# Weight preparation moved from ScalarE and GpSimd to VectorE, query and key rows normalised by VectorE out of PSUM, and the narrow branch of TensorE placed first

## The chip, the cores and the metric

The kernel runs on one core of a Trainium2 chip. The metric is the device time of one execution in microseconds (us). The kernel before takes 264.18 us (median of 3 runs, 264.0 to 264.33).

## The reference

Inputs are `x` (16 tiles of 128 rows by 256) and a context of the same shape. Two steps, each added to `x` with a tanh gate:

```
q = layernorm(x) @ Wq.T;  k, v = context @ Wk.T, context @ Wv.T interleaved    # 32 heads of 8
q, k = rmsnorm(q), rmsnorm(k)                    # per row and head, over 8 elements
x = x + tanh(g_xattn) * softmax(q k.T / sqrt(8)) v
h = layernorm(x);  W = (wq - 128) * scale        # int32 weights of gate, up (704x256), down (256x704)
x = x + tanh(g_ffn) * (silu(h Wg.T) * (h Wu.T)) Wd.T
```

## The kernel before

Each engine has a program of its own, in a fixed order, with semaphores between them. The unit of work is an iteration `p` (from -1 to 9), which carries two attention tiles and one pair of tiles of the feed-forward part; each iteration has a half `e = 0` and a half `e = 1`. Iterations 2 to 5 are a hardware loop, the others are written out. In iteration `p` the queries and keys of tiles 2p+2 and 2p+3 are made (iterations -1 to 6), the attention of tiles 2p and 2p+1 is done, and the feed-forward part of the pair p-2 is finished (chunks 2 to 5 of the hidden layer, then the two output products y0 and y1) and that of the pair p-1 begun (chunks 0 and 1).

**PSUM banks.** All projections share three banks. The order in which tasks take them is `TASKS` (L95), and the bank is in `BANK_OF` (L93):

```
BANK_OF = {"out0": 0, "v0": 1, "qk0": 2, "ffn2": 0, "ffn3": 1, "ffn4": 2, "ffn5": 0,
           "out1": 1, "v1": 2, "qk1": 0, "turn2": 1, "y0": 2, "y1": 0, "ffn0": 1, "ffn1": 2}
```

TensorE claims a bank with `claim` (L1071): it waits on `drained[k]` until every earlier task of that bank has been read out. So ffn4 follows qk0 in bank 2, and y1 follows qk1 in bank 0. Where the feed-forward tasks do not exist yet (iterations -1, 0 and 1), v1 follows qk0 in bank 2. In iteration 2 v0 follows ffn0 in bank 1 and qk0 follows ffn1 in bank 2.

**Queries and keys.** TensorE fills a bank with 512 columns (`queries_keys`, L1141). ScalarE squares it (`square`, L583) and copies it to SBUF (`copy_qk`, L594), which drains the bank. VectorE sums the squares per head (L842), runs a chain of eight small root instructions (L809, L736 to L742), and multiplies the copy with the roots into `qk_parts[:, :, 0]` in float16 (`qk_upper`, L855). GpSimd makes the same product in float32 (`qk_norm`, L451) and subtracts the float16 part (`split_qk`, L411) for the lower part. VectorE duplicates the parts (`qk_double`, L867 to L869), and the SP queue turns them with two DMA transposes (L340).

**Feed-forward weights.** They are int32 numbers less 128, kept as a float32r upper part (`gu_hi`, `dn_hi`) and a lower part (`gu_lo`, `dn_lo`) that only the wide branch uses. ScalarE makes the upper parts in iteration 0 (L513, L520, L522) and squares all weights for their maximum in iteration 1 (L535). GpSimd makes the lower parts in iterations 0 and 1 (L460, L462, L472, L474), in front of `add_attention` (L428), which adds the attention to `x` and on whose result VectorE's second layernorm waits (`statistics2`, L905). VectorE reduces the maxima (L973), a DMA turns them into a row (L372), and VectorE writes the flag `wide` (L980). TensorE loads the flag into a register after the attention of iteration 1 and branches (L1302 to L1311): the wide branch comes first in the code, the narrow one is the `Else`. With these inputs the narrow one runs: 8 matmuls for each full chunk.

`roots`, `gate`, `up` and `normalize2` are interleaved on VectorE by hand (L998 to L1062): in half 0, roots 1 to 5, gate 2, root 6, up 2, root 7, gate 3, up 3, then `qk_upper`; in half 1, roots 1 to 4, `turn2_lo` (L943), roots 5 to 7, `normalize2` (L827), then `qk_upper`.

## Time and profile before

| | us |
|---|---|
| median of 3 runs | 264.18 |
| profiled execution | 263.58 |
| its span, first to last instruction | 261.8 |
| TensorE busy | 206.6 (79%) |
| VectorE busy | 172.0 (66%) |
| ScalarE busy | 152.8 (58%) |
| GpSimd busy | 133.0 (51%) |

The profile shows one execution. Times in its rows count from the first instruction. PE is TensorE's matmuls, PEld its weight loads, DVE VectorE, ACT ScalarE, POOL GpSimd, SPq the queue of the DMA issues. The mean granted clock of TensorE is 0.909 of full speed.

### The profile page before, as it was taken

What the parts mean: (1) busy time and instruction counts of PE and PEld (TensorE: products, weight loads), DVE (VectorE), ACT (ScalarE), POOL (GpSimd) and SP (SyncE); (2) the same over time, 40 slices, a digit from 0 to 9 for tenths busy, and PEclk for the clock granted to TensorE, in tenths of its full rate; (3) what the DMA queues carried; (4) which work ended last, traced back from release to release, by engine and by line L of the source; (5) the groups of instructions that cost most, each with busy time, mean ns of one, the idle gap of its engine ahead of it and who ended that gap; (6) DMA issues with size and microseconds to landing.
All of it is one profiled execution on the core that took longest, in us unless ns stands there. A gap on an engine that the chain in (4) does not pass through costs nothing.

```text
span 261.8 us, 6738 instructions
## 1 busy us (share of the span) xinstructions
PE 206.6 (79%) x2388; PEld 162.0 (62%) x2388; DVE 172.0 (66%) x523; ACT 152.8 (58%) x284; POOL 133.0 (51%) x165
## 2 busy tenths in 40 slices
PE   3652966866700899989998999899999999886794
PEld 2441644544500777777777778687877877675784
DVE  2664163787080349795977788687959798576563
ACT  1122477676620378666856775687578767753371
POOL 5043079325929535464728382836375465444472
PEclk9995779596865599999999999999999999999799
DMA  7897505053500050616051605332351405010011
GB/s 235 248 341 170 123 0 123 0 42 82 120 1 3 4 123 0 72 50 160 0 120 21 140 5 115 64 96 49 72 124 44 80 3 123 0 43 1 3 40 40
DMA packets 44021, 20.15 MB, mean 77 GB/s; under 512 B 36384, under 2 KB 41440, under 8 KB 43872
## 3 DMA queue, kind: packets, MB, share of 16 engines
q1 hardware_dynamic: 44000, 19.87, 32.9%
q8 instruction: 13, 0.21, 0.3%
q14 instruction: 8, 0.07, 0.1%
HBM read 9.38 MB, written 2.10 MB: 44 GB/s over the span
## 4 chain that ended last, share of the span: by engine, by line
PE 40%; DVE 27%; issue 10%; POOL 9%; ACT 5%; DMA 5%; SPq 1%; DVEq 1%; POOLq 0%; ACTq 0%
PE bank L1130 10%; PE bank L1225 9%; PE bank L1203 8%; PE pv_ps L1112 7%; DVE silu L918 3%; POOL whole L460 3%; PE score_ps L1093 3%; DMA k_stack<-qk_parts 3%; POOL gu_lo L462 3%; ACT probs L549 3%; DVE hidden L933 2%; DVE sums L842 2%; PE bank L1185 1%; ACT squares L583 1%; POOL qk_parts L411 1%
## 5 line engine op out<-in xcount | busy, mean ns | idle before, releaser
L549 ACT ACTIVATE probs<-score_ps 128x1024 f32<-128x1024 f32 x64 | 64.6, 1023 | 9.7 <-PE score_ps L1093 9.3
L1203 PE MATMUL bank<-x_hi,gu_hi 128*128 128x256 f32 (+1 forms) x192 | 49.4, 294 | 14.4 <-issue 12.9
L451 POOL TENSOR_TENSOR qk_unit<-qk_raw,root_y 128x512 f32<-128x512 f32 x16 | 18.2, 1140 | 78.9 <-DVE root_y L742 78.9
L1112 PE MATMUL pv_ps<-probs,v_blocks 128*32 128x128 f32 x1024 | 43.4, 290 | 13.2 <-ACT probs L549 13.2
L1203 PE MATMUL bank<-x_lo,gu_hi 128*128 128x256 f32 (+1 forms) x192 | 47.5, 284 | 0.0
L1203 PEld LDWEIGHTS bank<-x_hi,gu_hi 128*128 128x128 f32 (+1 forms) x192 | 35.4, 184 | 18.1 <-issue 15.5
L419 POOL TENSOR_TENSOR h_lo<-hidden,h_hi 128x256 fp32r<-128x256 f32 (+1 forms) x48 | 37.3, 788 | 17.5 <-ACT h_hi L633 16.6
L1130 PE MATMUL bank<-w,xc 128*128 128x256 f32 x128 | 41.0, 474 | 5.5 <-DMA w<-qkv_dram 4.4
L622 ACT ACTIVATE tanh_g<-bank,half_gate 128x256 f32<-128x256 f32 (+1 forms) x48 | 22.7, 474 | 29.2 <-PE bank L1203 27.4
L1112 PEld LDWEIGHTS pv_ps<-probs,v_blocks 128*32 128x32 f32 x1024 | 25.3, 113 | 23.2 <-ACT probs L549 14.3
L1130 PEld LDWEIGHTS bank<-w,xc 128*128 128x128 f32 x128 | 28.6, 236 | 14.3 <-issue 7.3
L1203 PEld LDWEIGHTS bank<-x_lo,gu_hi 128*128 128x128 f32 (+1 forms) x192 | 35.5, 185 | 0.0
L918 DVE SCALAR_TENSOR_TENSOR silu<-tanh_g,bank 128x256 f32<-128x256 f32 (+1 forms) x48 | 19.9, 415 | 15.6 <-ACT tanh_g L622 15.4
L1093 PE MATMUL score_ps<-q_stack,k_stack 32*128 32x128 f16 x512 | 22.5, 227 | 8.5 <-DMA k_stack<-qk_parts 8.5
L1093 PEld LDWEIGHTS score_ps<-q_stack,k_stack 32*128 32x128 f16 x512 | 12.8, 97 | 19.8 <-DMA k_stack<-qk_parts 9.2
L905 DVE BATCH_NORM_STATS2 x_stats<-x_all 128x6 f32<-128x256 f32 (+1 forms) x16 | 6.8, 427 | 27.3 <-POOL x_all L428 27.3
L933 DVE SCALAR_TENSOR_TENSOR hidden<-silu,scales,bank 128x256 f32<-128x256 f32 (+1 forms) x48 | 23.0, 479 | 2.6
L1225 PE MATMUL bank<-dn_hi,h_hi 128*128 128x256 f32 x84 | 23.2, 310 | 0.1
L411 POOL TENSOR_TENSOR qk_parts<-qk_unit,qk_parts 128x512 f16<-128x512 f32 x16 | 18.9, 1179 | 7.8 <-DVE qk_parts L855 7.5
L1225 PE MATMUL bank<-dn_hi,h_lo 128*128 128x256 f32 x84 | 21.7, 293 | 0.0
L633 ACT CAST h_hi<-hidden 128x256 fp32r<-128x256 f32 (+1 forms) x48 | 18.2, 404 | 5.7 <-DVE hidden L933 5.1
L842 DVE TENSOR_REDUCE sums<-squares 128x64 f32<-128x512 f32 x16 | 11.0, 686 | 13.0 <-ACT squares L583 12.3
(93 smaller groups left out, 349.2 us busy)
## 6 DMA issues: line engine op xcount, KB each, us to landing
xc<-turned_dram SPq DMA_DIRECT2D x16, 256.0 KB, 2.9
out_dram<-x_all SPq DMA_DIRECT2D x16, 128.0 KB, 1.9
x_all<-x_dram SPq DMA_DIRECT2D x1, 1536.0 KB, 10.6
gu_int<-gate_up_dram SPq DMA_DIRECT2D x1, 1280.0 KB, 5.9
w<-qkv_dram SPq DMA_DIRECT2D x3, 256.0 KB, 3.4
dn_int<-down_w_dram SPq DMA_DIRECT2D x1, 640.0 KB, 7.1
x_all<-x_dram SPq DMA_DIRECT2D x1, 384.0 KB, 5.1
q_stack<-qk_parts SPq DMA_TRANSPOSE x16, 3.2
```

The lines of the kernel that those rows point to most:

```text
L411: nc.gpsimd.tensor_tensor(qk_parts[:, :, 1, :], qk_unit[:], qk_parts[:, :, 0, :], ALU.subtract).then_inc(qk_lo_ready, 1)
L419: nc.gpsimd.tensor_tensor(h_lo[0:r, j, :], hidden[0:r, j % 3, :], h_hi[0:r, j, :].bitcast(F32), ALU.subtract).then_inc(h_lo_ready, 1)
L451: nc.gpsimd.tensor_tensor(qk_unit[:], qk_raw[:], root_y[:, 0:2 * H].unsqueeze(2).to_broadcast([P, 2 * H, HD]), ALU.mult).then_inc(unit_rea ...
L549: nc.scalar.activation(probs[:, t % 2, :], score_ps[t % 2][:].rearrange("p h n -> p (h n)"), ACT.Exp, scale=float(HD) ** 0.5 / UNIT ** 2). ...
L622: nc.scalar.activation(tanh_g[0:r, j % 2, :], bank[k][0:r, 0:TOK], ACT.Tanh, scale=half_gate[0:r, j:j + 1]).then_inc(tanh_g_ready, 1)
L918: nc.vector.scalar_tensor_tensor(out=silu2[0:r, j % 2, :], in0=tanh_g[0:r, j % 2, :], scalar=1.0, in1=bank[k][0:r, 0:TOK], op0=ALU.add, op ...
L933: nc.vector.scalar_tensor_tensor(out=hidden[0:r, j % 3, :], in0=silu2[0:r, j % 2, :], scalar=scales[0:r, 2, j:j + 1], in1=bank[k][0:r, TOK ...
L1093: last = nc.tensor.matmul(score_ps[t % 2][:, s, :], k_stack[of, e, g, :], q_stack[of, e, g, :], start=True, stop=True, tile_position=(BLOC ...
L1112: last = nc.tensor.matmul(pv_ps[BLOCK * quadrant:BLOCK * (quadrant + 1), region * P:(region + 1) * P], v_blocks[:, e, h * BLOCK:(h + 1) * ...
L1130: last = nc.tensor.matmul(dst, xc[:, tile, source, c, :], weights[:, c, :], start=(c == 0), stop=(c == KC - 1))
L1203: last = nc.tensor.matmul(bank[k][0:r, a * TOK:(a + 1) * TOK], w[:, j, a, c, 0:r], xx[:, c, :], start=(n == 1), stop=(n == (4 if wide_weig ...
L1225: last = nc.tensor.matmul(bank[k][:, 0:D], hh[:, j, e * P:(e + 1) * P], w[:, j, :], start=(n == 1), stop=(n == (4 if wide_weights else 2) ...
```

## The change

- VectorE makes the product of queries and keys with the roots once, in float32, reading the PSUM bank (`qk_rows`), in the place where `qk_upper` stood; this instruction now drains the bank. `copy_qk`, `qk_norm` and the buffer `qk_raw` go. ScalarE copies the result to float16 (new `qk_upper`), in half 0 behind tanh of chunk 4, in half 1 behind `drain_y(p, 1)`. GpSimd only subtracts.
- All weight work but the squares is VectorE's. Upper parts: chunks 0 to 2 around `qk_rows(-1, 1)`, chunks 3 to 5 and the down weights in `begin(0)`. Lower parts: one fused instruction each instead of two, chunks 0 to 3 in iteration 0, 4 and 5 in iteration 1 behind `qk_rows`, the down weights in iteration 1 in front of `gate(1, 0)`. The squares stay on ScalarE, and all six run at the end of iteration -1.
- The maximum and the flag are made in `begin(0)`, its DMA is issued in iteration 0 behind `stacks(0, 0)`. The load of `x` tiles 4 to 15 moves behind iteration -1 of the SP queue.
- TensorE's branch has the narrow case first.

```diff
@@ SP
-            sp.dma_start(x_all[:, 4:B, :], x[4:B].rearrange("b p d -> p b d")).then_inc(x_loaded[2], 16)
+            def load_widest():
+                sp.wait_ge(w_max_steps, 1)
+                sp.dma_start(weight_max_row[:], weight_max[:, 6:7]).then_inc(w_max_row_loaded, 16)
             def iteration(p):
                 stacks(p, 0)
+                if p == 0:
+                    load_widest()
...
                 load_rows(p, 0)
-                if p == 1:
...
+                if p == FIRST:
+                    sp.dma_start(x_all[:, 4:B, :], x[4:B].rearrange("b p d -> p b d")).then_inc(x_loaded[2], 16)
@@ GpSimd
                 pool.wait_ge(qk_hi_ready, b + 3)
-                pool.wait_ge(unit_ready, b + 3)
                 nc.gpsimd.tensor_tensor(qk_parts[:, :, 1, :], qk_unit[:], qk_parts[:, :, 0, :],
@@ GpSimd, iteration
-                qk_norm(p, 0)
                 split_chunks(p, 2, (2,))
                 split_qk(p, 0)
                 split_chunks(p, 2, (3, 4, 5))
-                if isinstance(p, int) and p in (0, 1):
-                    for j in range(3 * p, 3 * p + 3):
-                        lower_gate_up(j)
                 add_attention(p, 1)
-                qk_norm(p, 1)
                 split_qk(p, 1)
-                if isinstance(p, int) and p == 1:
-                    for i in range(4):
-                        lower_down(i)
@@ ScalarE
-            def copy_qk(p, e):
+            def qk_upper(p, e):
...
-                    act.wait_ge(filled[k], m)
+                    act.wait_ge(drained[k], m)
                     if since(b, -1):
-                        act.wait_ge(unit_ready, b + 2)
-                        act.wait_ge(qk_hi_ready, b + 2)
-                    nc.scalar.copy(qk_raw[:].rearrange("p h d -> p (h d)"), bank[k][:]).then_inc(drained[k], 1)
+                        act.wait_ge(stacked, 32 * (b + 2))
+                    nc.scalar.copy(qk_parts[:, :, 0, :], qk_unit[:]).then_inc(qk_hi_ready, 1)
@@ ScalarE, iteration
                 square(p, 0)
                 exp_octet(p, 0, 2)
-                copy_qk(p, 0)
...
                 tanh_chunk(p, 2, 4)
                 if ending(p):
                     upper(p, 2, 3)
+                qk_upper(p, 0)
                 drain_pv(p, 1)
                 exp_octet(p, 1, 0)
...
                 square(p, 1)
-                copy_qk(p, 1)
+                if isinstance(p, int) and p == FIRST:
+                    act.wait_ge(rest_zeroed, 1)
+                    for i in range(6):
+                        square_weights(i)
...
                 exp_octet(p, 1, 3)
                 drain_y(p, 1)
+                qk_upper(p, 1)
                 tanh_chunk(p, 1, 0)
@@ VectorE
-            def qk_upper(p, e):
+            def qk_rows(p, e):
...
                 dve.wait_ge(root_steps, (ROOT_STEPS + 1) * (b + 3))
-                k, m = use(p, f"qk{e}")
-                dve.wait_ge(drained[k], m)
                 if since(b, -1):
-                    dve.wait_ge(stacked, 32 * (b + 2))
-                nc.vector.tensor_tensor(qk_parts[:, :, 0, :], qk_raw[:], root_y[:, 0:2 * H].unsqueeze(2).to_broadcast([P, 2 * H, HD]),
-                                        ALU.mult).then_inc(qk_hi_ready, 1)
+                    dve.wait_ge(qk_lo_ready, b + 2)
+                k, _ = use(p, f"qk{e}")
+                nc.vector.tensor_tensor(qk_unit[:], bank[k][:].rearrange("p (h d) -> p h d", d=HD),
+                                        root_y[:, 0:2 * H].unsqueeze(2).to_broadcast([P, 2 * H, HD]),
+                                        ALU.mult).then_inc(drained[k], 1)
+            def convert_gate_up(j):
...
+                nc.vector.tensor_scalar(gu_hi[:, j, :, :, 0:rows(j)], source, ZERO_POINT, None,
+                                        ALU.subtract).then_inc(gu_hi_ready, 1)
+            def convert_down():
...
+                for j0, j1, r in DOWN_PARTS:
+                    nc.vector.tensor_scalar(dn_hi[0:r, j0:j1, :], dn_int[0:r, j0:j1, :], ZERO_POINT, None,
+                                            ALU.subtract).then_inc(dn_hi_ready, 1)
+            def lower_gate_up(j):
...
+                nc.vector.scalar_tensor_tensor(out=gu_lo[:, j, :, :, 0:rows(j)], in0=source, scalar=-ZERO_POINT,
+                                               in1=gu_hi[:, j, :, :, 0:rows(j)].bitcast(F32), op0=ALU.add,
+                                               op1=ALU.subtract).then_inc(lo_ready, 1)
@@ VectorE, begin and iteration
+                if isinstance(p, int) and p == 0:
+                    widest_weight()
+                    for j in (3, 4, 5):
+                        convert_gate_up(j)
+                    any_wide_weight()
+                    convert_down()
...
-                qk_upper(p, 0)
+                qk_rows(p, 0)
+                if second:
+                    lower_gate_up(0)
+                    lower_gate_up(1)
+                if third:
+                    lower_gate_up(4)
+                    lower_gate_up(5)
...
-                qk_upper(p, 1)
+                if first:
+                    convert_gate_up(0)
+                    convert_gate_up(1)
+                qk_rows(p, 1)
+                if first:
+                    convert_gate_up(2)
                 if second:
-                    x_statistics(2, 10, B)
-                    x_means(3)
...
+                    lower_gate_up(2)
+                    lower_gate_up(3)
+                if third:
+                    qk_double(p, 2)
+                    for i in range(4):
+                        lower_down(i)
                 gate(p, 1, 0)
@@ TensorE
-            with pe.If_ne(any_wide, 0):
+            with pe.If_eq(any_wide, 0):
+                first_chunks(1, False)
+                run(pe, lambda p: iteration(p, False), FIRST_STEADY)
+            with pe.Else():
                 first_chunks(1, True)
                 run(pe, lambda p: iteration(p, True), FIRST_STEADY)
-            with pe.Else():
-                first_chunks(1, False)
-                run(pe, lambda p: iteration(p, False), FIRST_STEADY)
```

In iteration 0 (`second`) the statistics of tiles 10 to 15 move behind `qk_double(p, 2)`. `wait_for_root_buffers` waits on the drained bank where it waited on `unit_ready`.

## Rows read from the trace of the kernel before

**Rows 1.** Busy time by window, one steady period: window, length, engines' busy us (count), PEclk, DMA, GB/s.

```profile
117.55:142.25 24.70, 23.60 (x302) 18.74 (x298) 19.74 (x56) 17.77 (x34) 13.67 (x17) 1.00 0.34 74
```

**Rows 2.** The chain that ended last, in order of time: start us, us, what.

```profile
11.71 0.70 DVE sums L842
14.81 1.58 POOL qk_unit L451
...
81.02 4.63 issue
85.65 3.75 PE bank L1203 x16
...
95.83 0.61 ACT squares L583
...
112.80 1.88 PE bank L1203 x16
```

**Rows 3.** Timeline of PE, iteration 3: start us, us, what.

```profile
124.22 0.38 PE L1203 MATMUL bank<-x_hi,gu_hi 128*128 128x256 f32 x1
...
135.82 0.39 PE L1225 MATMUL bank<-dn_hi,h_hi 128*128 128x256 f32 x1
```

**Rows 4.** Timeline of ACT, iteration 3.

```profile
120.53 0.60 ACT L583 ACTIVATE squares<-bank 128x512 f32<-128x512 f32 x1 [0.59 <-PE bank L1130]
...
121.94 0.59 ACT L594 COPY qk_raw<-bank 128x512 f32<-128x512 f32 x1
```

**Rows 5.** Timeline of DVE, iteration 3.

```profile
125.78 1.09 DVE L855 TENSOR_TENSOR qk_parts<-qk_raw,root_y 128x512 f16<-128x512 f32 x1
...
133.38 0.69 DVE L842 TENSOR_REDUCE sums<-squares 128x64 f32<-128x512 f32 x1
...
137.21 1.28 DVE L827 TENSOR_SCALAR x1n<-x_all,x_mean_var,root_y 128x256 f32 x1
138.41 0.68 DVE L855 TENSOR_TENSOR qk_parts<-qk_raw,root_y 128x512 f16<-128x512 f32 x1
```

**Rows 6.** One line's or one tile's instructions: duration ns min/median/max, first and last start.

```profile
L943 DVE TENSOR_TENSOR x_lo<-bank,x_hi x8: 683/691/692, 75.2 to 246.3; 128x512 fp32r<-128x512 f32 x8
L827 DVE TENSOR_SCALAR x1n<-x_all,x_mean_var,root_y x16: 401/826/1277, 50.6 to 243.1; 128x256 f32<-128x256 f32 x8, 128x256 f32 x8
L535 ACT ACTIVATE weight_squares<-gu_int x3: 622/1075/1080, 56.4 to 62.9; 128x1024 f32<-128x1024 int32 x2, 128x512 f32<-128x512 int32 x1
L535 ACT ACTIVATE weight_squares<-dn_int x2: 407/845/1283, 69.4 to 70.7; 128x1280 f32<-128x1280 int32 x1, 64x256 f32<-64x256 int32 x1
```

**Rows 7.** Timeline of POOL up to 72 us.

```profile
36.13 1.16 POOL L411 TENSOR_TENSOR qk_parts<-qk_unit,qk_parts 128x512 f16<-128x512 f32 x1
...
71.60 0.73 POOL L428 TENSOR_TENSOR x_all<-x_all,attn 128x256 f32<-128x256 f32 x1
```

**Rows 8.** Timeline of PE up to 75 us.

```profile
12.21 3.78 PE L1130 MATMUL bank<-w,xc 128*128 128x256 f32 x8 [1.16 <-ACT qk_raw L594]
15.78 1.09 PE L1130 MATMUL bank<-wq_centred,xc 128*128 128x256 f32 x4
...
72.14 0.65 PE L1112 MATMUL pv_ps<-probs,v_blocks 128*32 128x128 f32 x16 [2.05 <-ACT probs L549]
```

**Rows 9.** Waits of one engine for another: us in total, times, longest.

```profile
DVE wide_max L978 <- DMA weight_max_row<-weight_max: 2.0, 1, 2.0
```

**Rows 10.** Timeline of SP's queue.

```profile
25.84 1.23 SPq L340 DMA_TRANSPOSE q_stack<-qk_parts  x1
```

**Rows 11.** Busy time by window, as in Rows 1, around two low stretches of TensorE.

```profile
59.00:61.00 2.00, 0.20 (x8) 0.00 (x0) 1.76 (x8) 0.91 (x3) 0.00 (x0) 0.82 0.82 196
...
72.00:73.00 1.00, 0.65 (x16) 0.38 (x16) 0.60 (x2) 1.00 (x3) 0.34 (x1) 1.00 0.02 8
```

**Rows 12.** Timeline of the end, all engines.

```profile
257.89 0.28 PE L1243 MATMUL bank<-dn_hi,h_lo 128*128 128x256 f32 x1
...
259.15 0.81 SPq L361 DMA_DIRECT2D out_dram<-x_all  x2
```

More of the change, by code:

```diff
@@ L142, in build_program @@
         dn_int = sb("dn_int", [P, NJ, D], I32)
-        whole = sb("whole", [P, 2 * D])
         gu_hi = sb("gu_hi", [P, NJ, 2, KC, P], F32R)
@@ L532, in square_weights @@
                              (LAST, dn_int[0:LAST, NJ - 1, :]))[i]
+                if i == 0:
+                    act.wait_ge(ffn_w_loaded[0], 16 * 2)
+                if i == 4:
+                    act.wait_ge(ffn_w_loaded[1], 16 * 2)
                 if i > 1:
@@ L661, in iteration @@
             def iteration(p):
-                def early(q, work, *args):
-                    if isinstance(p, int) and p == q:
-                        work(*args)
                 square(p, 0)
                 exp_octet(p, 0, 2)
-                copy_qk(p, 0)
-                early(0, convert_gate_up, 0)
-                early(1, square_weights, 0)
                 if not (isinstance(p, int) and p == PAIRS + 1):
@@ L774, in _, with wait_for_root_buffers @@
             x_means(0)
-            def wait_for_root_buffers(p, b):
+            def wait_for_root_buffers(p, e):
+                b = 2 * p + e
                 if has_tile(p, b - 1):
@@ L780, in wait_for_root_buffers @@
                 if since(b, -1) and has_tile(p, b + 1):
-                    dve.wait_ge(unit_ready, b + 2)
+                    k, m = use(p, "qk0") if e else use(p - 1, "qk1")
+                    dve.wait_ge(drained[k], m)
                 if since(b, 2):
@@ L791, in root_inputs @@
                 if not has_tile(p, b + 2):
-                    wait_for_root_buffers(p, b)
+                    wait_for_root_buffers(p, e)
                 if has_tile(p, b - 1):
@@ L968, in scale_setup, with lower_down @@
                 nc.vector.tensor_scalar(down_scale[:], down_scale[:], tanh_gates[:, 1:2], None, ALU.mult).then_inc(scale_steps, 1)
+            def convert_gate_up(j):
+                if j == 0:
+                    dve.wait_ge(ffn_w_loaded[0], 16 * 2)
+                source = gu_int[:, j] if j < NJ - 1 else gu_int_rest[:]
+                nc.vector.tensor_scalar(gu_hi[:, j, :, :, 0:rows(j)], source, ZERO_POINT, None,
+                                        ALU.subtract).then_inc(gu_hi_ready, 1)
+            def convert_down():
+                dve.wait_ge(ffn_w_loaded[1], 16 * 2)
+                dve.wait_ge(rest_zeroed, 1)
+                for j0, j1, r in DOWN_PARTS:
+                    nc.vector.tensor_scalar(dn_hi[0:r, j0:j1, :], dn_int[0:r, j0:j1, :], ZERO_POINT, None,
+                                            ALU.subtract).then_inc(dn_hi_ready, 1)
+            def lower_gate_up(j):
+                source = gu_int[:, j] if j < NJ - 1 else gu_int_rest[:]
+                dve.wait_ge(gu_hi_ready, j + 1)
+                nc.vector.scalar_tensor_tensor(out=gu_lo[:, j, :, :, 0:rows(j)], in0=source, scalar=-ZERO_POINT,
+                                               in1=gu_hi[:, j, :, :, 0:rows(j)].bitcast(F32), op0=ALU.add,
+                                               op1=ALU.subtract).then_inc(lo_ready, 1)
+            def lower_down(i):
+                j0, j1, r = DOWN_PARTS[i]
+                dve.wait_ge(dn_hi_ready, i + 1)
+                nc.vector.scalar_tensor_tensor(out=dn_lo[0:r, j0:j1, :], in0=dn_int[0:r, j0:j1, :], scalar=-ZERO_POINT,
+                                               in1=dn_hi[0:r, j0:j1, :].bitcast(F32), op0=ALU.add,
+                                               op1=ALU.subtract).then_inc(lo_ready, 1)
             def widest_weight():
@@ L1001, in iteration @@
                 second = isinstance(p, int) and p == FIRST + 1
+                third = isinstance(p, int) and p == 1
                 sum_squares(p, 0)
@@ L1060, in iteration @@
                 up(p, 1, 1)
-                qk_double(p, 2)
+                if not third:
+                    qk_double(p, 2)
+                if second:
+                    x_statistics(2, 10, B)
+                    x_means(3)
                 begin(p + 1)
```

69 lines of the change are left out of this document (3 added, 66 removed).

## The prediction

> **What bounds the kernel now.** I read the page first (engine shares), then busy time by window, then the chain of waits, then the timelines of single engines. Two regimes show. From iteration 2 on TensorE is the bound: in a steady period of 24.70 us it is busy 23.60 us at full granted clock, while VectorE works 19.74, ScalarE 17.77 and GpSimd 13.67 [rows 1]. Little can be hidden from TensorE there: 1.1 us. Up to 95.8 us the bound is latency. The chain has 4.63 us of "issue" from 81.02 to 85.65, when TensorE, done with the attention of iteration 1 at 72.8 [rows 8], has its flag and takes the branch [rows 2]; the first two chunks behind it run slow, 3.75 us for 16 matmuls that take 1.88 later [rows 2]. Before that, GpSimd's weight work holds back `add_attention`, to 71.60 in iteration 1 [rows 7].
>
> So the change has two sums: what it saves up to the point where ScalarE squares the queries and keys of iteration 2, now at 95.83 [rows 2], and what it adds to each of the five iterations 2 to 6 that make queries and keys beside the feed-forward part.
>
> **Steady iterations, half 0.** Today ScalarE's copy frees the bank of qk0 at 121.94 + 0.59 = 122.53 [rows 4]. The next task of that bank is ffn4, and TensorE begins it at 124.22 [rows 3], 1.7 us later: the bank is never waited for. After the change `qk_rows` frees it, and it needs the whole root chain. It stands where `qk_upper` stands, at 125.78 [rows 5]. VectorE works without a gap from the sums to there, and nothing before it becomes shorter. Its duration: a product of 512 columns with one operand in PSUM takes 0.69 (x_lo [rows 6]); today's `qk_upper` from SBUF takes 0.68 undisturbed and 1.09 here [rows 5], where GpSimd works beside it. I take 0.69, as x_lo is 0.69 at all 8 places; the bounds are 0.68 and 1.09. The bank is free at 126.47, ffn4 begins at 126.5 and not 124.22: +2.28 us (bounds 2.2 to 2.7). Everything behind it on TensorE's queue moves: attention of the next tile, ffn5, v1 and qk1, and so ScalarE's square of qk1 from 131.69 to 133.97. The cover that copy_qk gave is gone and nothing takes its place, since TensorE executes in order.
>
> **Steady iterations, half 1.** qk1 frees bank 0 for y1, which begins at 135.82 [rows 3]; with +2.28 that is 138.1. The VectorE side: ScalarE's upper copy of half 0 runs behind tanh of chunk 4, about 128.2 to 128.8 (a 512-column copy is 0.59 [rows 4]), GpSimd's subtraction to 130.0 (1.16 [rows 7]). gate and up of chunk 5, the three doubling copies, the division and GpSimd's addition of the attention follow, and the sums begin at about 135.1, not 133.38 [rows 5]: less than +2.28 later, as VectorE lagged by some 0.5 there. From the sums to the end of the roots 3.83 pass (133.38 to 137.21 [rows 5], with turn2_lo inside). Then the normalisation: 1.28 today, beside GpSimd's float32 product, 0.40 undisturbed [rows 5, 6]; that product is gone, so 0.40. `qk_rows(p, 1)` runs at 139.3 to 140.0, and y1 begins at 140.05: another +1.9 us (bounds 1.3 to 2.8, the upper one if the normalisation keeps 1.28). ScalarE's copy of half 1 fits in the 0.6 us between draining y1 and the tanh of chunk 0. The transposes start within 1 us of where they do now relative to the period, 5 us ahead of the scores that need them. The period becomes 24.70 + 2.28 + 1.9 = 28.9 us. Over five iterations: 5 x 4.16 = +20.8 us (bounds 18 to 25). The rest, iterations 7 to 9, has no qk tasks and keeps its length.
>
> **The first iterations.** Here each engine's queue has to be followed; every time below is the largest of what the instruction waits for, with durations of before. A root chain without normalisation is 3.1 from sums to product [rows 2].
> - Iteration -1: qk0 is full at 11.0 as now, the product runs 14.76 to 15.45. v1 needs that bank: TensorE starts it at 15.5, not 12.21 [rows 8]. Behind the idle time the 12 matmuls are mostly slow (8 took 3.57, the next 4 1.09 [rows 8]): qk1 is full at about 20.5. ScalarE squares it and then all weights, six instructions and their accumulator reads, 4.8 us (1.075 x 2 + 0.62 + 0.40 + 1.28 + 0.41 less overlap, [rows 6]), to 25.8. VectorE: sums 21.15, roots 24.15, two conversions. A one-operand conversion of 512 columns from int32 is in no row on VectorE; bounds 0.40 (the 256-column normalisation, undisturbed) and 0.69 [rows 6]; I take 0.55. `qk_rows(-1, 1)` ends near 26.0, ScalarE's copy at 26.6, and only then comes the first exp, at 26.6 in place of 23.9.
> - Iteration 0: qk0 full at 33.3. On VectorE `begin(0)` stands in front of its sums: the doubling ends at 28.5, conversions to 30.2, then the flag's DMA, which SP issues behind two transposes (1.23 each and more [rows 10]) at 31.1 and which takes 2.0 [rows 9] (behind the landing of the transposes up to 2 more): 33.2, then the flag and four conversions to 35.9. Sums 2 us late, product to 39.65. ScalarE waits with its upper copy for it, and behind the copy in its queue stand the drain of pv and the exps of tile 1: exp at 40.65. v1 and qk1: full at 47.3. In return GpSimd's addition follows the division at once (47.1), and sums(0, 1) start at 48.0. The product ends at 52.35, ScalarE copies to 53.0, and the exps of iteration 1 stand behind that: 53.35. qk0 of iteration 1 full at 60.0, the product at 64.6, exps of the second tile at 65.6, qk1 full at 72.0.
> - Iteration 1, end: the attention was added long before (69.2, today 72.3 [rows 7]), so sums(1, 1) start at 72.75, today 72.83. turn2_lo ends at 75.9 and chunk 0 can start there: the flag has been known since 34. Were the 4.63 of load and branch paid in full from 74.2, it would be 78.8; the narrow case now follows the branch directly, so I take 76. The product ends at 77.7, copy 78.35, subtraction 79.55, doubling 80.2, and then four lower parts of the down weights, 0.69 x 2 + 0.41 x 2 = 2.2 (two operands, as x_lo; bound above 1.49 each, were they as slow as GpSimd, +3): gate 0 at 82.4, up 0 to 83.3, up 1 to 84.2. v0 of iteration 2 waits for bank 1 (up 0), qk0 for bank 2 (up 1): full at 86.4.
>
> So the square of iteration 2 comes at 86.4 in place of 95.83: -9.4 us. The 10 us saved at chunk 0 are not more than this since VectorE's lower parts stand in front of gate 0. A slow clock or a slow branch at 76 is hidden behind them. Bounds -6 (conversions and lower parts at the dear end, flag late) to -12.
>
> **The end.** The narrow body now has the wide one behind it, and TensorE has to jump over it after its last matmul at 258.2 [rows 12]. At the price of today's jump, 4.63 [rows 2], it ends at 262.8, against 261.8 for the last store, whose issue is at 259.15 and later [rows 12]: +1.0 (bounds 0 and 1.0).
>
> **Sum.** 263.58 (profiled execution) - 9.4 + 20.8 + 1.0 = 276.0. The median of the runs is 0.6 above the profiled one, which is in the rounding: 276 us.
>
> **Rivals.**
> - *The stalls cost the clock.* After each stall TensorE may run at 1.2 GHz. For it: the clock was granted at 0.82 on average in 59 to 61, with 0.20 us of work there [rows 11]. Against: after the 2.05 us idle up to 72.14 the products run in 0.65 and the granted clock is 1.00 [rows 8, 11], and dense matmuls stand on both sides of my stalls of 2.3 and 1.9. Price: 16 matmuls lose 1.87 [rows 2]; one fall per iteration makes 276 + 9.4 = 285, two make 295. The Trainium skill, "TensorE: Matmul & The Clock Gate", section "Why this matters for your kernels", wants no idle gap over about 3 us between bursts; by that rule neither stall would cost the clock, and the time stays 276. The trace agrees with it at 72.14; at 59 to 61 the clock fell behind gaps of about 2 us in a thin stretch, which the rule does not tell.
> - *The stalls are hidden (the other side).* If ffn4 and y1 met a free bank, only the start and the end would count: 263.58 - 9.4 + 1.0 = 255. The mechanism would be a shorter VectorE chain, with GpSimd's product gone. The point from which it decides is a stall of 1.7 us per iteration in all: (9.4 - 1.0) / 5. For it: VectorE loses up to 0.9 us per half to GpSimd's work beside it. Against: that contention lies behind the sums only in half 1, where I have taken it out; in half 0 the gap from 122.53 to 126.47 is 3.9 us and TensorE has 1.7 us of slack.
> - *The first iterations gain nothing.* ScalarE's upper copy waits for VectorE in front of the exps, and all its delays add up in iterations -1 to 1: were the four steps each 2 us dearer, chunk 0 would come at 84 and the time would be 285.
>
> **How the numbers follow.** Forecast 0.68, clock 0.13, hidden stalls 0.06, no gain at the start 0.07; 0.06 for what I have not seen, spread over both sides. Own range of the forecast: all cheap ends together give 263.58 - 12 + 18 + 0 = 270, all dear ones 263.58 - 6 + 25 + 1 = 284; as they will hardly meet, 271 to 282. For 8 in 10 I widen it to 268 to 285, up to the first clock fall. A change within 0.2% (0.5 us) cannot be told from none. Faster takes the hidden stalls and a little of the rest, 0.06; same 0.02; slower 0.92.
>
> **What would show it.** The wait of ffn4 and of y1 on `qk_rows` as idle time of TensorE of some 2 us each in iterations 2 to 6, and a period near 28.9 between their qk0. Chunk 0 at about 76, the square of iteration 2 near 86, no "issue" of 4.6 in front of it, and such a piece at the end. ScalarE's exps of iterations 0 and 1 right behind its upper copies. Granted clock 1.00 from iteration 2 on. It is wrong if the period stays below 26.4 us, or if the square of iteration 2 comes before 83 or after 91.

## The result and the profile after

| | before | after |
|---|---|---|
| median of the runs | 264.09 us (263.96 to 264.33) | 281.78 us (279.6 to 282.53) |
| profiled execution / its span | 263.58 / 261.8 us | 282.23 / 280.4 us |
| ScalarE's square of q and k, iteration 2 | 95.83 | 84.83 |
| the same, iterations 3 to 6 | 120.53, 145.24, 169.92, 194.31 | 114.03, 144.75, 175.37, 205.65 |

The changed kernel takes 1.0655 [1.0594, 1.0717] times as long: slower, by 17.7 us. The forecast was 276.0 (268 to 285), so the time lies inside the range, 5.8 us above the forecast.

The two rows of the page of the changed kernel that say most, busy time and the clock by slice:

```profile
PE 212.9 (76%) x2388; PEld 166.2 (59%) x2388; DVE 166.3 (59%) x543; ACT 149.0 (53%) x276; POOL 88.7 (32%) x129
PEclk9997777687889999979997999989997979999799
```

GpSimd, which the change relieves, shows it (88.7 us busy in place of 133.0), and so does something that I did not forecast: slices with clock digit 7 in the steady part, where the kernel before has 9 throughout. By period of the changed kernel (window, length, engines' busy us, clock), to hold against [rows 1]:

```profile
84.83:114.03 29.20, 23.51 (x306) 18.82 (x300) 17.36 (x55) 17.61 (x34) 11.20 (x16) 1.00 0.20 41
114.03:144.75 30.72, 25.02 (x306) 19.93 (x300) 17.38 (x55) 17.92 (x34) 10.90 (x15) 0.94 0.27 60
144.75:175.37 30.62, 24.93 (x306) 19.84 (x300) 17.41 (x55) 17.91 (x33) 10.88 (x15) 0.94 0.29 59
175.37:205.65 30.28, 24.80 (x302) 19.67 (x298) 17.40 (x55) 17.91 (x33) 10.81 (x15) 0.94 0.27 57
```

The first period has full clock and is 4.5 us longer than before, all of it idle time of TensorE: 5.7 us of it here, 1.1 in [rows 1]. The next three have 1.1 to 1.5 us on top, and in them TensorE is *busy* 1.3 to 1.5 us longer with the same work. So a period pays twice: for two waits, and for a clock fall. The waits of the changed kernel (who waits at which line <- for whom: us in total, times, longest):

```profile
PE bank L1211 <- DVE qk_unit L785: 12.6, 5, 2.6
PE bank L1189 <- DVE qk_unit L785: 11.1, 5, 2.2
PE bank L1116 <- DVE qk_unit L785: 4.5, 1, 4.5
DVE wide_max L941 <- DMA weight_max_row<-weight_max: 4.0, 1, 4.0
```

L1189 is ffn4, L1211 is y1, both waiting for `qk_rows`; L1116 is v1 of iteration -1. What VectorE did up to the release, in iteration 4 (its timeline):

```profile
150.01 0.68 DVE L785 TENSOR_TENSOR qk_unit<-bank,root_y 128x512 f32<-128x512 f32 x1
...
164.98 0.41 DVE L758 TENSOR_SCALAR x1n<-x_all,x_mean_var,root_y 128x256 f32 x1
165.31 0.68 DVE L785 TENSOR_TENSOR qk_unit<-bank,root_y 128x512 f32<-128x512 f32 x1
```

and TensorE at the same places, with iteration 2 ahead of it:

```profile
90.83 0.39 PE L1189 MATMUL bank<-x_hi,gu_hi 128*128 128x256 f32 x1 [2.24 <-DVE qk_unit L785]
91.94 0.64 PE L1098 MATMUL pv_ps<-probs,v_blocks 128*32 128x128 f32 x16
...
150.75 0.56 PE L1189 MATMUL bank<-x_hi,gu_hi 128*128 128x256 f32 x1 [2.24 <-DVE qk_unit L785]
152.73 1.08 PE L1098 MATMUL pv_ps<-probs,v_blocks 128*32 128x128 f32 x16
...
166.05 0.39 PE L1211 MATMUL bank<-dn_hi,h_hi 128*128 128x256 f32 x1 [2.60 <-DVE qk_unit L785]
```

The product takes 0.68 reading PSUM, the normalisation 0.41 in place of 1.28 [rows 5]. Both waits of 2.24 us are alike, but behind that of iteration 2 the 16 small products (one row, x16) take 0.64 and behind that of iteration 4 they take 1.08. The granted clock in the 2 us behind each wait (windows of the changed kernel; the third number from the end is the clock), ffn4 and y1 of iterations 2, 3 and 6:

```profile
90.83:92.83 2.00, 2.00 (x32) 1.58 (x32) 0.47 (x2) 0.71 (x2) 0.00 (x0) 1.00 0.00 0
104.61:106.61 2.00, 2.00 (x17) 2.00 (x18) 0.00 (x0) 0.21 (x1) 0.00 (x0) 1.00 0.00 0
120.03:122.03 2.00, 2.00 (x10) 1.77 (x10) 0.27 (x1) 0.00 (x0) 0.00 (x0) 0.51 0.00 0
135.33:137.33 2.00, 2.00 (x17) 2.00 (x18) 0.00 (x0) 0.21 (x1) 0.00 (x0) 1.00 0.00 0
...
211.60:213.60 2.00, 2.00 (x20) 1.75 (x24) 0.27 (x1) 0.39 (x2) 0.00 (x0) 0.66 0.00 0
226.44:228.44 2.00, 2.00 (x9) 2.00 (x10) 0.00 (x0) 0.00 (x0) 0.00 (x0) 0.50 0.00 0
```

0.5 is the 1.2 GHz level. It falls behind ffn4's wait in iterations 3 to 6 and behind y1's in iteration 6 alone. (Behind ffn4 of iteration 6 it falls within the 2 us, hence 0.66.)

**The account of 280.4 - 261.8 = 18.6 us**, from the squares in the table: start -11.0; periods of iterations 2 to 5 +4.50, +6.01, +5.94, +5.89; from the square of iteration 6 to the attention product that opens iteration 7 +7.17 (25.56, before 18.39); the rest +0.1.

The first iterations and the end, on TensorE, VectorE and ScalarE of the changed kernel:

```profile
75.08 0.36 PE L1189 MATMUL bank<-x_hi,gu_hi 128*128 128x256 f32 x1 [1.70 <-DVE x_lo L874]
...
78.23 1.05 PE L1098 MATMUL pv_ps<-probs,v_blocks 128*32 128x128 f32 x16
81.02 0.64 PE L1098 MATMUL pv_ps<-probs,v_blocks 128*32 128x128 f32 x16 [0.51 <-ACT probs L492]
```

```profile
24.96 0.76 DVE L906 TENSOR_SCALAR gu_hi<-gu_int 128x512 fp32r<-128x512 int32 x2
...
78.94 1.95 DVE L929 SCALAR_TENSOR_TENSOR dn_lo<-dn_int,dn_hi 128x512 fp32r<-128x512 int32 x4
80.82 0.40 DVE L849 SCALAR_TENSOR_TENSOR silu<-tanh_g,bank 128x256 f32<-128x256 f32 x1
81.25 0.48 DVE L864 SCALAR_TENSOR_TENSOR hidden<-silu,scales,bank 128x256 f32<-128x256 f32 x1
```

```profile
39.23 0.62 ACT L536 CAST qk_parts<-qk_unit 128x512 f16<-128x512 f32 x1 [3.68 <-DVE qk_unit L785]
...
79.74 1.95 ACT L492 ACTIVATE probs<-score_ps 128x1024 f32<-128x1024 f32 x2
...
84.83 0.60 ACT L526 ACTIVATE squares<-bank 128x512 f32<-128x512 f32 x1 [0.65 <-PE bank L1116]
```

```profile
276.69 0.76 DVE L883 TENSOR_TENSOR y_sb<-bank,down_scale 128x256 f32<-128x256 f32 x2 [2.04 <-PE bank L1229]
```

Chunk 0 begins at 75.08 in place of 85.65 [rows 2], waiting for x_lo and for no branch. The wait of 4.0 us for the flag's DMA, shown above, delays VectorE's sums of iteration 0 (35.47, where ScalarE's square was done at 33.71), and ScalarE, whose upper copy now needs the product behind these sums, stands idle for 3.68 us in front of it, with the drain of the attention and the exps of the next tile behind. At the end the last drain begins at 276.69 and the span ends 3.7 us later; before, it was 3.8 (258.0 to 261.8): TensorE's jump over the second body shows nowhere.

### The profile page after: what moved, and what is told of

The parts are those of the page before. It is cut to its first block, busy times and chain, and to the rows that moved or that the text cites. A ratio compares the mean times of both kernels' runs of the same rounds, so it can differ in the third digit from the quotient of the medians.

```text
span 280.4 us, 6665 instructions
## 1 busy us (share of the span) xinstructions
PE 212.9 (76%) x2388; PEld 166.2 (59%) x2388; DVE 166.3 (59%) x543; ACT 149.0 (53%) x276; POOL 88.7 (32%) x129
## 4 chain that ended last, share of the span: by engine, by line
PE 28%; issue 28%; DVE 24%; POOL 9%; ACT 7%; DMA 2%; DVEq 1%; POOLq 0%; SPq 0%; ACTq 0%
PE bank L1116 9%; PE bank L1211 6%; PE bank L1189 5%; POOL h_lo L421 4%; PE pv_ps L1098 4%; POOL x_all L430 2%; DVE silu L849 2%; DVE qk_unit L785 2%; DVE sums L773 2%; POOL qk_parts L413 2%; ACT probs L492 2%; DVE hidden L864 2%; DMA w<-qkv_dram 2%; ACT weight_squares L478 1%; DVE attn L826 1%
## 5 line engine op out<-in xcount | busy, mean ns | idle before, releaser
L1189 PE MATMUL bank<-x_hi,gu_hi 128*128 128x256 f32 (+1 forms) x192 | 51.8, 304 | 14.2 <-DVE qk_unit L785 11.1
L1098 PE MATMUL pv_ps<-probs,v_blocks 128*32 128x128 f32 x1024 | 45.1, 299 | 9.7 <-ACT probs L492 9.6
L1189 PE MATMUL bank<-x_lo,gu_hi 128*128 128x256 f32 (+1 forms) x192 | 49.8, 294 | 0.0
L421 POOL TENSOR_TENSOR h_lo<-hidden,h_hi 128x256 fp32r<-128x256 f32 (+1 forms) x48 | 34.4, 728 | 45.6 <-ACT h_hi L575 45.4
L1189 PEld LDWEIGHTS bank<-x_hi,gu_hi 128*128 128x128 f32 (+1 forms) x192 | 37.0, 193 | 18.6 <-DVE qk_unit L785 12.4
L1116 PE MATMUL bank<-w,xc 128*128 128x256 f32 x128 | 40.0, 464 | 8.8 <-DVE qk_unit L785 4.5
L1116 PEld LDWEIGHTS bank<-w,xc 128*128 128x128 f32 x128 | 27.9, 231 | 17.5 <-DVE qk_unit L785 5.2
L1189 PEld LDWEIGHTS bank<-x_lo,gu_hi 128*128 128x128 f32 (+1 forms) x192 | 37.4, 195 | 0.0
L1211 PE MATMUL bank<-dn_hi,h_hi 128*128 128x256 f32 x84 | 24.2, 321 | 12.7 <-DVE qk_unit L785 12.6
L1211 PEld LDWEIGHTS bank<-dn_hi,h_hi 128*128 128x128 f32 x84 | 17.4, 207 | 16.1 <-DVE qk_unit L785 13.9
L1211 PE MATMUL bank<-dn_hi,h_lo 128*128 128x256 f32 x84 | 22.4, 300 | 0.0
L549 ACT COPY y_sb<-bank 128x256 f32<-128x256 f32 x14 | 5.2, 373 | 28.5 <-PE bank L1211 28.5
```

Of the source, the lines that this page charges most:

```text
L421: nc.gpsimd.tensor_tensor(h_lo[0:r, j, :], hidden[0:r, j % 3, :], h_hi[0:r, j, :].bitcast(F32), ALU.subtract).then_inc(h_lo_ready, 1)
L1098: last = nc.tensor.matmul(pv_ps[BLOCK * quadrant:BLOCK * (quadrant + 1), region * P:(region + 1) * P], v_blocks[:, e, h * BLOCK:(h + 1) * ...
L1116: last = nc.tensor.matmul(dst, xc[:, tile, source, c, :], weights[:, c, :], start=(c == 0), stop=(c == KC - 1))
L1189: last = nc.tensor.matmul(bank[k][0:r, a * TOK:(a + 1) * TOK], w[:, j, a, c, 0:r], xx[:, c, :], start=(n == 1), stop=(n == (4 if wide_weig ...
L1211: last = nc.tensor.matmul(bank[k][:, 0:D], hh[:, j, e * P:(e + 1) * P], w[:, j, :], start=(n == 1), stop=(n == (4 if wide_weights else 2) ...
```

## Experiments

Each time is a median of four executions with the lowest and the highest, and the ratio is to the kernel before, measured beside it: 264.03 us beside the first four, 263.24 beside the next four, 263.67 beside the last two. The changed kernel's 281.78 was measured beside 264.09, so a difference to it is uncertain by the 0.8 us that the kernel before moved, besides the spread of the runs. Traces show one execution each. Line numbers differ a little from kernel to kernel.

**1. Take one path back: ScalarE drains the bank again.**

```diff
+ScalarE: copy_qk(p, e): wait filled; qk_raw <- bank; drained += 1   # shortened, as in the edits below
 def qk_rows(p, e):
-    qk_unit <- bank[k] * root_y      # then_inc(drained[k])
+    qk_unit <- qk_raw * root_y       # then_inc(unit_ready)
```

> The changed kernel, but ScalarE again copies queries and keys out of PSUM and drains the bank (where it did before), and qk_rows reads the copy; ScalarE's float16 copy stays. Theory 'bank': TensorE's two waits per iteration (2.2 and 2.2 to 2.6 us, iterations 2 to 6) and the granted clock below 1.00 behind them come from the bank that qk_rows frees late. Then they all go: periods of 24.7 us again, 281.8 - 22.3 (four periods) - 7.2 (iteration 6) = 252 us, and v1 of iteration -1 starts 3 us earlier, so 248 to 254. Rival 'queue': the longer period comes from ScalarE's upper copy, which waits for VectorE in front of other work in ScalarE's queue. Then the copy back changes little, 275 to 285, and the periods stay near 30.

Measured: 251.64 us (250.22 to 253.37), 0.9517 [0.9446, 0.9588]. Its periods from 83.51 on (windows), and VectorE's product in one of them:

```profile
83.51:108.25 24.74, 23.31 (x306) 18.64 (x300) 17.31 (x55) 18.33 (x35) 10.54 (x15) 1.00 0.21 41
108.25:133.25 25.00, 23.48 (x306) 18.80 (x300) 17.81 (x56) 18.42 (x35) 10.96 (x15) 1.00 0.34 76
```

```profile
138.50 0.90 DVE L798 TENSOR_TENSOR qk_unit<-qk_raw,root_y 128x512 f32<-128x512 f32 x1
```

The period is back at 24.6 to 25.0 and the clock at 1.00, with VectorE still making the rows, the product still behind the roots, and ScalarE's upper copy still waiting for it (15 times, 20.1 us in all). So the loss of the steady part is neither VectorE's load nor the order of its queue: it is when the bank comes free, and the clock falls hang on the same waits.

**2. The branch alone** (the kernel before, with the narrow body first).

```diff
-with pe.If_ne(any_wide, 0):  wide body
-with pe.Else():              narrow body
+with pe.If_eq(any_wide, 0):  narrow body
+with pe.Else():              wide body
```

> The kernel before with the narrow branch first and nothing else. Theory 'jump': of the 4.63 us between flag and first chunk most is the taken branch. Then chunk 0 starts at about 81.5 in place of 85.65 and the time is about 260 us, with nothing given back at the end (the changed kernel shows 3.7 us from the last y_sb product to the end, as the kernel before does 3.8). Rival 'load': the 4.63 is the register load from SBUF and the branch costs little. Then 264 us as before.

Measured: 259.98 us (259.12 to 260.51), 0.9841 [0.9779, 0.9903]. The chain of work that ended last, in order of time:

```profile
80.65 1.98 DMA weight_max_row<-weight_max
83.11 1.04 issue
84.16 3.46 PE bank L1203 x16
```

From the end of the flag's DMA to the first matmul 1.5 us pass (82.63 to 84.16); before, they were 5.1, the 4.63 of [rows 2] and some 0.5 ahead of it. The order of two bodies is worth 3.6 us there, 4.1 in the median (the interval of the ratio lies wholly below 1), and nothing of it is given back at the end: from the last drain to the end 3.7 us pass. The Trainium skill, "Runtime: NRT & Kernel Launch", section "Instruction fetch mechanics", says that a taken branch to code outside the window already fetched makes the engine wait for a fetch. The 3.6 us agree with it; that it is a fetch, no row here shows.

**3. The weight work alone** (all of the change but the path of the query and key rows).

```diff
+POOL:    qk_norm(p, e): qk_unit <- qk_raw * root_y
+ScalarE: copy_qk(p, e): qk_raw <- bank; drained += 1
-ScalarE: qk_upper(p, e): qk_parts[.., 0] <- qk_unit
 VectorE, in qk_rows(p, e):
-    qk_unit <- bank[k] * root_y
+    qk_parts[.., 0] <- qk_raw * root_y
```

> All of the change but the path of queries and keys: weight work on VectorE, squares early, flag early, narrow branch first, with ScalarE's copy, VectorE's float16 product and GpSimd's float32 product as before. Theory 'bank': the gain of the first iterations (11.0 us in the changed kernel up to the square of iteration 2) stays and nothing is lost afterwards: 264.1 - 11 = 253, a little less as v1 of iteration -1 need not wait: 249 to 254 us. If the gain at the start needs the new path (GpSimd and ScalarE less loaded), it is smaller: 256 to 260.

Measured: 249.8 us (248.78 to 251.84), 0.9485 [0.941, 0.9561]. One period of it:

```profile
106.52:131.10 24.58, 23.47 (x306) 18.61 (x300) 19.75 (x56) 17.77 (x33) 13.93 (x18) 1.00 0.37 79
```

The square of iteration 2 comes at 81.80, the period is that of before. This is the version to keep: it beats both kernels, by 14.2 and by 32 us. (Experiment 1 at 251.64 lies close to it; their runs overlap.)

**4. The query and key path alone** (the kernel before with `qk_rows` and the upper copy on ScalarE; GpSimd's weight work and the wide body first stay).

```diff
-POOL: qk_norm(p, e)          ScalarE: copy_qk(p, e)
+VectorE: qk_rows(p, e)       ScalarE: qk_upper(p, e)
```

> The kernel before with the new path of queries and keys only (VectorE's product out of PSUM, ScalarE's upper copy, GpSimd subtracts); weight work and branch as before. Theory 'bank': the loss of iterations 2 to 6 is all here, 22.3 + 7.2 = 29.5 us, and iterations -1 to 1 lose some more by v1's wait for the bank: 292 to 299 us. Theory 'queue' gives the same here; it is told apart by the kernel with the copy back.

Measured: 294.67 us (292.0 to 296.16), 1.1184 [1.1102, 1.1266]: +30.6 us. With the -14.2 of experiment 3 the parts add up to 280.4, against 281.8 measured for both. One part gains 14, the other loses 31. Its first two periods are 29.13 and 30.58 us, as in the changed kernel. I had expected the first iterations to lose some more by v1's wait. In the trace (an execution of 292.0 us, the fastest of the four) they do not: the square of iteration 2 comes at 95.94, before at 95.83, and all of the loss lies behind it.

**5. Shorten one of the two waits.** In half 0 VectorE had the gate and up of chunk 3 between the roots and the product.

```diff
                     roots(p, 0, 7, 7)
+                    qk_rows(p, 0)
                     gate(p, 2, 3)
                     up(p, 2, 3)
-                qk_rows(p, 0)
```

> The changed kernel with qk_rows(p, 0) directly behind root 7, in front of gate 3 and up 3 of chunk 3 (0.84 us of VectorE). Theory 'bank': TensorE's wait in front of chunk 4 falls from 2.24 to 1.4 us in iterations 2 to 6, -4.2 us: 277.5 us if the clock still falls behind it. If that wait was what let the clock fall (chunk 4 in 1.98 us against 1.14), the slow stretch goes too, another 1.5 us in four of the iterations: 271 to 273. Rival 'VectorE's chain sets the period whatever the place': gate 3 and up 3 are only pushed behind, 280 to 282.

Measured: 276.73 us (276.2 to 277.42), 1.0503 [1.0444, 1.0562], 5.0 below the changed kernel. In the traces 2.4 us of this lie ahead of iteration 2, where the order of VectorE's work is unchanged: the square comes at 82.38 and not at 84.83, and no run shows why. From that square to the end 192.0 us pass and not 195.6, so the move is worth 3.6. TensorE at ffn4 and y1 of iteration 3, and the clock behind them:

```profile
116.19 0.38 PE L1191 MATMUL bank<-x_hi,gu_hi 128*128 128x256 f32 x1 [1.53 <-DVE qk_unit L785]
...
130.00 0.38 PE L1213 MATMUL bank<-dn_hi,h_hi 128*128 128x256 f32 x1 [2.60 <-DVE qk_unit L785]
```

```profile
116.19:118.19 2.00, 2.00 (x32) 1.60 (x32) 1.25 (x4) 0.68 (x2) 0.32 (x1) 1.00 0.00 0
130.00:132.00 2.00, 2.00 (x14) 2.00 (x15) 0.00 (x0) 0.00 (x0) 0.00 (x0) 0.78 0.00 0
```

The wait shrank by 0.7 us in each of the five iterations, which is all of the 3.6, as a term of the sum should. The clock gave nothing back, against the 271 to 273 us expected for that case. It no longer fell behind ffn4 in iterations 3 and 4, but it fell behind y1 in iterations 3, 5 and 6, and in iteration 5 behind ffn4 too (0.72, after a wait of 1.52); it fell behind neither in iterations 2 and 4. The periods are 28.5, 30.0, 28.4 and 32.4 us.

**6. Keep the waits, fill them.** Eight float32 matmuls of 128 x 128 into an unused part of PSUM in front of ffn4 and of y1; they add work that no output uses.

```diff
+                if j == 4 and has_tile(p, 2 * p + 2):
+                    fill(8)
                 k = claim(p, f"ffn{j}")
...
+                if e == 1 and has_tile(p, 2 * p + 3):
+                    fill(8)
                 k = claim(p, f"y{e}")
```

> The changed kernel with eight extra matmuls of TensorE (128x128 float32, into 128 columns of PSUM that nobody reads) in each of its two waits for qk_rows, in iterations 2 to 6. They take no bank and fit in the wait (about 8 x 0.14 to 0.2 us = 1.1 to 1.6 of 2.2 us). Theory 'clock': iterations 3 to 6 are 1.5 us longer than iteration 2 because the granted clock falls behind the wait. Then it stays at 1.00, chunk 4 takes 1.14 us, all periods are near 29.2: 281.8 - 1.5 x 4 - 1.4 = 274 to 275.5 us. Rival: the extra 1.5 us are another delay (a queue, a contention), then 281 to 283, or above where the extra matmuls don't fit.

Measured: 273.7 us (273.07 to 274.86), 1.0394 [1.0334, 1.0454]: 8.1 us *faster* than the changed kernel, with 80 matmuls more (each stands as two records in the trace). TensorE at the place of the wait, and two periods:

```profile
146.03 2.05 PE L1178 MATMUL pv_ps<-ident,averaging 128*128 128x128 f32 x16
148.34 0.39 PE L1197 MATMUL bank<-x_hi,gu_hi 128*128 128x256 f32 x1 [0.25 <-DVE qk_unit L786]
```

```profile
113.19:142.34 29.15, 27.41 (x338) 22.46 (x332) 17.43 (x55) 17.61 (x34) 10.90 (x15) 1.00 0.29 63
142.34:171.47 29.13, 27.40 (x338) 22.46 (x332) 17.42 (x55) 17.61 (x34) 10.90 (x15) 1.00 0.30 63
```

The first three periods are 29.13 to 29.15 us, the fourth 28.95, all at full clock. The eight products took 2.05 us, more than the 1.1 to 1.6 that I had expected, and still fit in the wait. The price of the waits without the clock is 29.14 - 24.70 = 4.4 us. The price of the clock is read from the two traces: from the square of iteration 2 to the opening of iteration 7 this kernel needs 7.3 us less (139.06, changed 146.38). The other 1.8 us between the spans (271.3 and 280.4) are no part of it: 0.8 lie ahead of that square, and 1.0 behind iteration 6, where the changed kernel has a late clock fall that the kernel before has too.

**7. The changed kernel with the wide body first again.** My prediction had said that a slow branch at 76 us would be hidden behind VectorE's lower parts.

```diff
-            with pe.If_eq(any_wide, 0):
+            with pe.If_ne(any_wide, 0):
```

> The changed kernel with the wide branch first again, as before the change, so that TensorE has to jump; the flag is still early. The kernel with the narrow branch first alone gained 4.1 us where the flag was late. Here the load and the jump begin at 72.8 us and chunk 0 would start near 77.4 in place of 75.1, at the lower clock. Theory 'hidden': gate 0 starts at 80.8 whatever TensorE does, as the lower parts of the down weights stand in front of it, so 281.8 to 282.5 us, no more than 0.5 us longer. Rival: all of the 4 us shows, 286.

Measured: 287.5 us (286.0 to 289.85), 1.0884 [1.0801, 1.0967]: 5.7 us slower than the changed kernel. "Hidden" falls. Its TensorE, ScalarE and VectorE around the branch:

```profile
78.51 0.55 PE L1189 MATMUL bank<-x_hi,gu_hi 128*128 128x256 f32 x1 [4.01 <-issue]
...
82.19 1.08 PE L1098 MATMUL pv_ps<-probs,v_blocks 128*32 128x128 f32 x16
...
85.13 0.64 PE L1098 MATMUL pv_ps<-probs,v_blocks 128*32 128x128 f32 x16 [0.64 <-ACT probs L492]
```

```profile
83.86 1.94 ACT L492 ACTIVATE probs<-score_ps 128x1024 f32<-128x1024 f32 x2
...
88.68 0.60 ACT L526 ACTIVATE squares<-bank 128x512 f32<-128x512 f32 x1 [0.59 <-PE bank L1116]
```

```profile
81.93 0.41 DVE L849 SCALAR_TENSOR_TENSOR silu<-tanh_g,bank 128x256 f32<-128x256 f32 x1
```

This run came to the branch 1.1 us later (ScalarE's last square ahead of it at 72.01, not 70.89). VectorE's gate 0 is later by just that (81.93 against 80.82): it did hide the branch. TensorE shows it all the same: it idles for 4.01 us in front of chunk 0, and the two chunks then take 3.7 us and not 3.1, as less of them runs at full clock. The attention product behind chunk 1 is 3.96 us later (82.19 against 78.23), the exps 4.1, the second product 4.1 (85.13 against 81.02), and the square 3.85. The path that shows is the one through TensorE's queue, attention behind two chunks, and I had not followed it. The two spans differ by 7.6 us (288.0 and 280.4; the profiled execution was the slowest of its four). Behind the square the first two periods are longer by another 4.2, 31.9 and 32.2 us at a mean clock of 0.89 (29.2 and 30.7 at 1.00 and 0.94 in the changed kernel): the clock falls again, in other places. The stretches behind them give 0.4 back.

**8. Move the flag's wait out of the way.** The weight work alone (experiment 3), with VectorE's last conversions and the wait for the flag's DMA behind the upper part of iteration 0.

```diff
 VectorE, iteration 0
-    convert(3..5), wait flag, convert_down      # in begin(0)
     ...
     qk_rows(0, 0)
-    lower_gate_up(0), (1)                       # now with (2), (3), in half 1
+    convert(3..5), wait flag, convert_down
```

> The kernel with the weight part only (249.8 us), and in it the conversions of chunks 3 to 5 and of the down weights and the wait for the flag's DMA behind VectorE's qk_upper(0, 0) in place of in front of the sums of iteration 0; the lower parts of chunks 0 and 1 move to those of 2 and 3. In the weight-only kernel the sums stand about 4 us behind ScalarE's squares there, waiting for the flag's DMA. If that wait is on the path it gains 2 to 3.5 us: 246.5 to 248. If iteration 0 is set by ScalarE's squares of the weights and the transposes instead, 249.5 to 250.

Measured: 250.34 us (249.42 to 250.68), 0.9482 [0.943, 0.9534], against 249.8 for experiment 3. No gain: VectorE's wait for the flag, 6.15 us in the kernel of experiment 3, is not on the path there. This does not carry over to the changed kernel, with its wait of 4.0 us: there ScalarE's exps stand behind the upper copy, which waits for VectorE. What its wait costs, no run shows.

**9. Fill only the wait of ffn4.**

> The changed kernel with 8 extra 128x128 products only in the first stall of an iteration (before ffn4), none in front of y1. The products add work that no output uses. In the changed kernel the clock fell to 1.2 GHz behind the first stall in four of five iterations and behind the second in one. Theory A (a fall belongs to the stall in front of it, the 2.6 us of the second stall is safe wherever it stands between dense products of 128 rows): the four falls of some 1.5 us go, 281.8 - 6 = 275.8, range 275 to 276.7, and the granted clock behind y1's stall stays 1.00 in iterations 2 to 5. Theory B (a stall of this length is at the edge, and which one falls hangs on where it lies in time): the falls move, behind y1's stall in two or more of the first four iterations, 277 to 281.

Measured: 282.45 us (279.88 to 282.79), 1.0674 [1.06, 1.0749]. Theory A falls altogether. Of theory B the sign came, falls behind y1 in two or more of the first four iterations, and the time did not: 282.45 lies above its 277 to 281. The 2 us behind y1's wait, iterations 2, 3, 4 and 6 of this kernel:

```profile
104.77:106.77 2.00, 2.00 (x17) 2.00 (x18) 0.00 (x0) 0.21 (x1) 0.00 (x0) 1.00 0.00 0
...
134.02:136.02 2.00, 2.00 (x9) 2.00 (x10) 0.00 (x0) 0.00 (x0) 0.00 (x0) 0.50 0.00 0
...
164.73:166.73 2.00, 2.00 (x9) 2.00 (x10) 0.00 (x0) 0.00 (x0) 0.00 (x0) 0.50 0.00 0
...
225.39:227.39 2.00, 2.00 (x12) 2.00 (x13) 0.00 (x0) 0.00 (x0) 0.00 (x0) 0.67 0.04 8
```

In iterations 3 to 5 each fall that no longer came behind ffn4 came behind y1 instead, 14 us later, and in iteration 6 y1's was hit as before; behind ffn4 the clock was 1.00 in iterations 2 to 5. So the wait of 2.6 us that looked safe in the changed kernel is not safe in itself. Nor does a fall behind ffn4 simply spare y1: in iteration 6 of the changed kernel both were hit, in iteration 2 neither.

**10. Fill only the wait of y1.**

> The changed kernel with 8 extra products only in the second stall (before y1), none in front of ffn4; they add work that no output uses. Theory A: the first stall's four falls stay, the one fall behind the second goes: 281.8 - 1.5 = 280.3, range 279.5 to 281. Theory B (the place in time decides): the falls behind the first stall come in other iterations, 1 to 5 of them, so anything from 276 to 282; two or fewer of the five would speak for B.

Measured: 279.96 us (279.03 to 281.69), 1.0614 [1.054, 1.0687]. The clock fell behind ffn4 in iterations 3 to 6 and behind y1 never. The time lies in A's range of 279.5 to 281 and in B's of 276 to 282, and it does not speak for A, since experiment 9 has refuted it; B's sign, two or fewer falls, did not come either. With both results, one open wait of 2.1 to 2.6 us per iteration is enough for one fall in each of iterations 3 to 6, and filling one of the two leaves four falls of five.

## Why the prediction was right, and where it missed

**Direction and mechanism: right.** The forecast waits of ffn4 and y1 on `qk_rows`, some 2 us each, came as 2.24 and 2.60 us; the square of iteration 2 came at 84.83 inside its window of 83 to 91; the period is far beyond 26.4. Experiments 1, 3 and 4 separate the two sums: +30.6 for one part alone, -14.2 for the other. They also answer two of the rivals: the stalls were not hidden (255 us), and the first iterations gained 11.0 us and not nothing (285 us).

**Steady part: the two waits.** Measured 4.50 per iteration at full clock, 4.16 forecast, so 22.3 over the five (4 x 4.50, and 4.3 in iteration 6, where they are 2.10 and 2.21) for 20.8. The durations were right (product 0.68, normalisation 0.41, and the 3.83 from sums to roots to the digit: 99.71 to 103.54); the sums of half 1 came 14.88 behind the square and not 14.57. VectorE had the attention ready at 96.99, but GpSimd, with three lower parts of the hidden chunks in front, added it only at 98.14. +1.5 us.

**Steady part: the clock, the term I had at zero.** "Granted clock 1.00 from iteration 2 on" was wrong in iterations 3 to 6. This was my first rival, at 0.13, and it happened in part: five falls of the ten waits, at 1.5, 1.4, 1.4 and, for the two of iteration 6, 2.9 us: 7.2 us in the account, 7.3 by the traces of experiment 6. I had priced one at 1.87. My argument against it was the full clock behind 2.05 us of idle time [rows 8, 11] and dense products on both sides. One row was a sample of one: the changed kernel itself shows a wait of 2.24 us without a fall (iteration 2) and with one (iterations 3 to 5). And the products right in front of both waits are attention products of 32 columns, as at 87.95 and 132.09, with dense ones only behind. Whether that matters, no run shows. The Trainium skill, "TensorE: Matmul & The Clock Gate", section "Why this matters for your kernels", which I had set beside this rival, wants no idle gap over about 3 us. None of these waits is over 2.6 us, and yet the clock fell in four of five iterations: the trace disagrees with the rule, and the measurement decides.

**The first iterations: -11.0, forecast -9.4.** Chunk 0 at 75.08 (forecast 76), no 4.6 us of issue. Conversions take 0.42 each and not 0.55, lower parts 0.68 as forecast; VectorE had the flag at 34.0, forecast 33.2. The 1.6 us beyond the forecast grew in small steps: ScalarE's squares came 0.2, 0.8, 0.6 and 1.1 us before the forecast in iterations 0 and 1, and 1.6 us before it in iteration 2. The step that failed is "A slow clock or a slow branch at 76 is hidden behind them". Experiment 7 shows 2.75 us at the square (3.85 less the 1.1 of the later start) for a branch of 4.0 us and the slower products behind it. In the changed kernel the two paths meet: VectorE's first `hidden` ends at 81.73, the attention product at 81.66. I had computed the first and called it the only one.

**The end: 0, forecast +1.0.** The price of the branch before chunk 0, 4.63 us, was carried over to the end without a row for it. From the last drain to the end 3.7 us pass, as before.

**Sum.** 276.0 + 1.5 + 7.2 - 1.6 - 1.0 + 0.1 = 282.2, the profiled execution's 282.23. That the time fell inside the range is partly luck. Without the clock the terms measured give 275.0 us, which is the forecast's own mechanism and nearly its number; 7.2 us came from a term that stood at zero. The range of 268 to 285 was widened up to the first clock fall, so it covered this; the inner range of 271 to 282 had no clock in it at all, and 281.8 lies in it only because it allowed for dear conversions, flags and waits that did not come.

## What to carry to other kernels

Look for what a drain of a PSUM bank really releases: the cheap copy of 0.6 us by another engine was not wasted work but what kept a 4-us chain of small VectorE operations off TensorE's path; removing it cost 31 us, while the rest of the change gained 14. A wait of 2 us that is added to a TensorE-bound loop should be priced with a clock fall on top, here about one per iteration and not one per wait: of ten waits five were hit, and of the five left by filling the others four. When a step is said to be hidden behind one engine, follow the other queues over the same stretch too, the delayed engine's own first.

## What the hardware showed that I had not expected

- The clock. Of ten waits of 2.1 to 2.6 us five were followed by a fall in the changed kernel; of the five left with y1's filled, four; of the five left with ffn4's filled, four; with both filled, none. Equal waits in equal surroundings differed (iteration 2 against 3). What decides which one is hit stays open. A wait of some 1.5 us (experiment 5) was not hit in three of four iterations, and in the fourth the clock was 0.72 behind it.
- More work made the kernel faster: 80 matmuls whose result nobody reads, -8.1 us between the medians; in the traces 7.3 us in the iterations with the waits.
- The order of two bodies behind a branch was worth 4.1 us before and 5.7 after (of these, in the traces, some 2.75 at the branch and the rest in slower iterations behind it); the jump at the end cost nothing that the rows show.
- VectorE read 512 float32 columns from PSUM with a broadcast operand in 0.68 to 0.69 us at all 16 places, while the same product from SBUF, in half 0 of the steady iterations, took 0.90 (experiment 1) and 1.09 before [rows 5]; in half 1 it took 0.68 to 0.69 from SBUF too. Reading PSUM directly was the dearer choice only through the bank that it kept.
